# Value windows and key tiles at one distance for all tiles, and five transfers per pair issued by ScalarE

## The reference

```python
# 1: neighbourhood attention, 16 heads of 8 channels, a 7 x 7 window clamped at the image's edges
xf  = ln_c(x).transpose(0, 2, 3, 1)
q, k, v = split(xf @ qkv_w.T);  q = q * 8 ** -0.5
si = clip(arange(56) - 3, 0, 49)          # first key row of query row i; sj likewise for columns
logits[i, j, a, c] = q[i, j] . k[si[i] + a, sj[j] + c] + rpb[si[i] + a - i + 6, sj[j] + c - j + 6]
x = x + (softmax(logits over a, c) @ v) @ proj_w.T + proj_b
# 2: mixture of experts on tokens: top 2 of 8 experts, hidden width 512, relu
t = tokens(x);  t = t + moe(ln_t(t))
```

## Time and profile before

| what | us |
|---|---|
| median of three runs (lowest, highest) | 3022.98 (3019.34, 3025.69) |
| the profiled execution: its own time | 3022.68 |
| the profiled execution: span from first to last instruction | 3020.9 |
| time around the span in it | 1.8 |
| PE busy over the span | 2688.8 (89%) |
| DVE, ACT, POOL busy over the span | 2269.4, 2114.3, 1583.9 |
| mean granted clock of PE over the span | 0.947 |

### The profile page before, as it was taken

One profiled execution on the slowest core, in us unless ns is written; L12 is line 12 of the kernel. 1 busy time (PEld: TensorE's weight loads), 2 busy tenths in 40 slices (PEclk: granted clock), 3 DMA queues, 4 the chain that ended last, 5 costly groups with the idle time before them and its releaser, 6 DMA issues. The chain is left out here.

```text
span 3020.9 us, 112796 instructions
## 1 busy us (share of the span) xinstructions
PE 2688.8 (89%) x31346; PEld 2395.9 (79%) x31451; DVE 2269.4 (75%) x12559; ACT 2114.3 (70%) x5724; POOL 1583.9 (52%) x2025
## 2 busy tenths in 40 slices
PE   4789999999999999999999999999939999999733
PEld 2789999899989998999899989999936766776522
DVE  2668888788878887888788868888857888888655
ACT  1567878787878886887787868888847777777500
POOL 2135555455545554555455545555565777777600
PEclk9999999999999999999999999999969999999855
DMA  2665666555546664656566645566645444444399
GB/s 48 153 122 124 129 124 123 112 122 127 126 102 130 124 124 102 130 128 124 101 127 128 129 99 124 125 125 129 132 91 105 97 94 97 97 94 97 101 323 322
DMA packets 714047, 378.50 MB, mean 125 GB/s; under 512 B 422528, under 2 KB 669984, under 8 KB 713504
## 3 DMA queue, kind: packets, MB, share of 16 engines
q1 hardware_dynamic: 660704, 235.97, 40.3%
q10 hardware_dynamic: 24192, 81.67, 9.5%
q0 software_dynamic: 28608, 54.48, 6.1%
HBM read 233.43 MB, written 98.11 MB: 110 GB/s over the span
## 5 line engine op out<-in xcount | busy, mean ns | idle before, releaser
L1061 ACT ACTIVATE pr<-sc,nmx 128x100 f32<-128x100 f32 x3136 | 923.9, 369 | 61.9 <-DVE nmx L678 60.9
L962 POOL TENSOR_TENSOR oml<-om 128x256 f16<-128x256 f32 x784 | 479.6, 612 | 907.3 <-DVE om L708 890.4
L533 PE MATMUL bank<-vwin,pt 100*128 100x65 f32 x6272 | 806.2, 272 | 36.3 <-DVE om L708 28.1
L678 DVE CUSTOM_DVE_ANT_0 sc<-bank,near 128x100 f32<-128x100 f32 x3136 | 633.5, 257 | 253.7 <-PE bank L511 207.8
L533 PEld LDWEIGHTS bank<-vwin,pt 100*128 100x128 f32 x6272 | 773.4, 194 | 54.3 <-ACT pt L1069 39.5
L511 PE MATMUL bank<-kimg,held 128*128 (+2 forms) x9408 | 628.2, 216 | 40.9 <-issue 22.9
L511 PEld LDWEIGHTS bank<-kimg,held 128*128 128x128 bf16 (+1 forms) x9408 | 561.3, 100 | 88.3 <-issue 56.7
L1069 ACT ACTIVATE pt<-bank 100x512 f32<-100x512 f32 x784 | 460.6, 587 | 223.5 <-PE bank L520 208.8
L1367 POOL DMA_INDIRECT yrows<-ye,meta x420 | 449.2, 1070 | 154.6 <-issue 109.8
L930 POOL DMA_INDIRECT xrows<-rows,idx x448 | 433.9, 969 | 114.9 <-issue 75.5
L520 PE MATMUL bank<-cst_sb,pr 128*100 128x128 f32 x3136 | 477.1, 275 | 0.0
(11 more groups left out here) (133 smaller groups left out, 3366.8 us busy)
## 6 DMA issues: line engine op xcount, KB each, us to landing
vwin<-v_pix SPq DMA_DIRECT2D x1120, 60.5 KB
near<-bias_rows ACTq DMA_DIRECT2D x112, 600.0 KB, 4.7
y<-yrows SPq DMA_DIRECT2D x112, 224.0 KB, 4.3
held<-qring SPq DMA_DIRECT2D x896, 14.0 KB
v_pix<-vrow SPq DMA_DIRECT2D x56, 225.8 KB
xin<-in_x SPq DMA_DIRECT2D x56, 224.0 KB
xres<-in_x SPq DMA_DIRECT2D x112, 112.0 KB
x<-xres SPq DMA_DIRECT2D x112, 112.0 KB
```

The lines of the kernel that those rows point to most:

```text
L533: mm = pe.matmul(ps_av[m % 2][:, 2 * t + blk, :], pt[:, m % 2, 2 * t + blk, :], vwin[:, st, 2 * u + t, 64 * blk:64 * blk + 65], start=True ...
L678: i = v.tensor_tensor_reduce(out=sc[:, ring(m, par), k, :], in0=ps_s[m % 2][:, k, :], in1=near[:, st, ct, k, :], scale=-1.0, scalar=-MASKE ...
L962: g.tensor_tensor(oml[:, st, u], om[:, st, u], om_h[:, st, u], ALU.subtract).then_inc(s["oml_done"], 1)
L1061: i = a.activation(pr[:, r, k, :], sc[:, r, k, :], ACT.Exp, bias=nmx[:, r, k:k + 1], scale=-1.0)
```

## The change

All 14 tiles of a strip get their keys at one distance: tile t begins at column 4 t - 3, also at the edges, where it then reaches three columns beyond the image's row. What it finds there (pixels of the neighbouring row, or zeros before the first and behind the last pixel of all) is masked: the mask tables and the offset into the bias table are changed so that the edge tiles' valid keys lie where they now fall. The key image `kimg` gets 4 columns before and behind, set to zero by four DVE memsets; `v_pix` gets 4 rows before and behind, set to zero by two POOL transfers. A strip's values come by ten transfers of 14 tiles in place of ten of 12 tiles and two for the edges.

Two stores of x1, two residual loads and one token load per pair leave SP's list and go to ACT's list at units 4, 7, 11 and 13, behind that unit's `exps` and routing steps. SP's list of a pair is put in a new order.

```diff
@@ windows (SP)
-                    at = ((J // NPAIR) * IMG + krow(J, st) * W) * VW
+                    at = ((J // NPAIR) * IMG + krow(J, st) * W + EDGE - 3) * VW
                     for kr in range(KW):
-                        src = bass.AP(v_pix.tensor, at + (kr * W + 1) * VW, [[VW, KW], [TS * VW, NTILE - 2], [1, VW]])
-                        sp.dma_start(vwin[kr * KW:(kr + 1) * KW, st, 1:NTILE - 1], src).then_inc(s[f"v_in{st}"], 16)
-                    for t, c0 in ((0, 0), (NTILE - 1, W - KW)):
-                        src = bass.AP(v_pix.tensor, at + c0 * VW, [[W * VW, KW], [VW, KW], [1, VW]])
-                        sp.dma_start(vwin[:, st, t], src).then_inc(s[f"v_in{st}"], 16)
+                        src = bass.AP(v_pix.tensor, at + kr * W * VW, [[VW, KW], [TS * VW, NTILE], [1, VW]])
+                        sp.dma_start(vwin[kr * KW:(kr + 1) * KW, st], src).then_inc(s[f"v_in{st}"], 16)
@@ body (SP), for a pair J
-                    if not early(J, 1):
-                        store_x1(J - 1, 0)
+                    if more:
+                        spread_q(J + 1, 1 - par)
                     if fetch:
                         load_x(I + 1)
                     windows(J, 1, tail and J == PAIRS - 1)
                     if more:
-                        spread_q(J + 1, 1 - par)
-                    if not early(J, 1):
-                        store_x1(J - 1, 1)
-                    load_res(J, 0)
-                    if more:
                         windows(J + 1, 0, tail)
-                    load_res(J, 1)
-                    if not early(J, 1):
-                        load_tokens(J - 1, 1 - par)
                     if I is not None:
                         store_v(I)
                     if isinstance(J, int) and J == 0:
                         ...
@@ scores (PE)
-                        k0 = min(max(TS * tile - 3, 0), W - KW)
+                        k0 = TS * tile - 3
@@ start of the lists of DVE and POOL
+                for part in range(2):
+                    for col in (0, EDGE + IMG):
+                        i = v.memset(kimg[:, part, col:col + EDGE], 0.0)
+                i.then_inc(s["k_edge"], 1)
+                g.wait_ge(s["null_done"], 2)
+                for px in (0, EDGE + B * IMG):
+                    g.dma_start(bass.AP(v_pix.tensor, px * VW, [[run, lines], [1, run]]), none[0:lines, 0:run]).then_inc(s["v_edge"], 16)
@@ bias tables (DVE) and masks
-                                    o_r, o_c = 6 - 3 * rt, 6 - 3 * tt
+                                    o_r, o_c = 6 - 3 * rt, 3
-                    r, c = lo(qr, rt), lo(qc, ct)
+                    r, c = lo(qr, rt), (KW - KSZ, qc, 0)[ct]
@@ body (ACT), at the end of unit m; load_res, store_x1 and load_tokens now wait and issue on ACT
+                            if early(J, 1):
+                                if m == 0:
+                                    load_res(J, 0)
+                                    load_res(J, 1)
+                            elif m == 4:
+                                store_x1(J - 1, 0)
+                            elif m == 7:
+                                load_res(J, 0)
+                            elif m == 11:
+                                store_x1(J - 1, 1)
+                            elif m == 13:
+                                load_res(J, 1)
+                                load_tokens(J - 1, 1 - par)
```

More of the change, by code:

```diff
@@ L81 @@
 NROW = PAIR // HALF
-WIN_DMAS = 16 * (KW + 2)
+WIN_DMAS = 16 * KW
+EDGE = 4
 def build(nc, x, qkv_w_t, rpb, proj_w_t, proj_b, w_router, w1, b1, w2, b2, cst, win, cst2, out):
@@ L103, in sem @@
             return ctx.enter_context(nc.semaphore(name))
-        v_pix = nc.dram_tensor("v_pix", (B * IMG, VW), FP32, kind="Internal").ap()
+        v_pix = nc.dram_tensor("v_pix", (B * IMG + 2 * EDGE, VW), FP32, kind="Internal").ap()
         bias_rows = nc.dram_tensor("bias_rows", (3, 128, 3 * 4 * NKEY), FP32, kind="Internal").ap()
@@ L147, in build @@
         near = asb("near", [128, 2, 3, 4, NKEY])
-        kimg = asb("kimg", [C, 2, IMG], BF16)
-        kimg_h, kimg_l = kimg[:, 0], kimg[:, 1].bitcast(FP16)
+        kimg = asb("kimg", [C, 2, IMG + 2 * EDGE], BF16)
+        kimg_h, kimg_l = kimg[:, 0, EDGE:EDGE + IMG], kimg[:, 1, EDGE:EDGE + IMG].bitcast(FP16)
         qring = asb("qring", [C, QRING * 2 * STRIP])
@@ L230, in build @@
             c_small r_small r_wrm r_const r_first r_x0 r_x1 r_t r_turned r_logit r_stat r_ve r_pow r_nmr r_lg r_top r_atf r_hot r_hots
-            r_gap r_gapr r_eg r_share r_gate r_pos r_prod r_idxf r_idx r_cap r_xn r_hi r_lo r_dest r_both r_sc0 r_sc1 w2_in split_h split1 split2 t_ready null_done null_in""".split()
+            r_gap r_gapr r_eg r_share r_gate r_pos r_prod r_idxf r_idx r_cap r_xn r_hi r_lo r_dest r_both r_sc0 r_sc1 v_edge k_edge w2_in split_h split1 split2 t_ready null_done null_in""".split()
         s = {n: sem(n) for n in names}
@@ L319, in store_v @@
                     sp.wait_ge(s["v_out"], I + 1)
-                    dst = bass.AP(v_pix.tensor, I * (PAIR * VW), [[VW, HALF], [HALF * VW, NROW], [1, VW]])
+                    dst = bass.AP(v_pix.tensor, (I * PAIR + EDGE) * VW, [[VW, HALF], [HALF * VW, NROW], [1, VW]])
                     sp.dma_start(dst, vrow[:]).then_inc(s["v_store"], 16)
@@ L379, in body @@
                         if I == 1:
+                            sp.wait_ge(s["v_edge"], 32)
                             windows(0, 0, False)
@@ L435, in _ @@
                 pe.wait_ge(s["zeroed"], 2)
+                pe.wait_ge(s["k_edge"], 1)
                 pe.wait_ge(s["c_small"], 32)
@@ L891, in _ @@
                 g.memset(lost[:], 0).then_inc(s["null_done"], 1)
+                g.wait_ge(s["null_done"], 2)
+                lines = 8 if EDGE * VW % 8 == 0 else 6
+                run = EDGE * VW // lines
+                for px in (0, EDGE + B * IMG):
+                    g.dma_start(bass.AP(v_pix.tensor, px * VW, [[run, lines], [1, run]]), none[0:lines, 0:run]).then_inc(s["v_edge"], 16)
                 g.memset(ahead[:], TOK)
@@ L1046, in near_bias, with load_res, store_x1, load_tokens @@
                     a.dma_start(near[:, st].rearrange("p c a k -> p (c a k)"), src).then_inc(s[f"near_in{st}"], 16)
+                def load_res(J, st):
+                    b = J // NPAIR
+                    if not (isinstance(J, int) and J == 0):
+                        a.wait_ge(s[f"x1_store{st}"], 16 * J)
+                    src = bass.AP(x.tensor, b * (C * IMG) + (J % NPAIR) * PAIR + st * STRIP, [[IMG, C], [1, STRIP]])
+                    a.dma_start(xres[:, st, :], src).then_inc(s[f"xres_in{st}"], 16)
+                def store_x1(J, st):
+                    a.wait_ge(s["proj_out"], 2 * J + st + 1)
+                    a.dma_start(x1[:, bass.ds(J * PAIR + st * STRIP, STRIP)], xres[:, st, :])\
+                        .then_inc(s[f"x1_store{st}"], 16)
+                def load_tokens(Q, par):
+                    if not early(Q, 2):
+                        a.wait_ge(s["r_logit"], Q - 1)
+                    a.dma_start(xt[:, par, :], x1[:, bass.ds(Q * PAIR, PAIR)]).then_inc(s[f"r_x{par}"], 16)
                 def exps(J, m, par):
```

## The result

| | before | after | ratio (95%) |
|---|---|---|---|
| median, us | 3024.34 | 3075.93 | 1.0144 (1.0115 to 1.0174) |
| profiled execution, us | 3022.68 | 3067.8 | |
| its span, us | 3020.9 | 3066.0 | |

The forecast was 3030, its range ended at 3047. The sign was right, the size was not: +45.1 us of span between the two profiled executions (+51.6 between the medians), where +7.0 was summed.

The account below looks back on a forecast made before the run. PE's own list was taken to bound the loop, with SP late only at J = 1. The terms, +6.1 us at J = 1 and +0.9 at J = 0, the rest 0, gave +7.0 and 3030.0 us, range 3018 to 3047.

Parts of the forecast that it names:

- Part 2: Five issues per pair moved from SP to ACT in stage 1: 0 us, bounds 0 and 94 us.
- I take a landing under 5 us and no wait: At unit 13, the x1 store issued at unit 11 lands before ACT's residual load needs it, 5.1 us later: 0 us.
- Part 3: SP's new order, spread first: 0 in the loop, +6.1 us at J = 1, +0.9 us at J = 0.
- ACT is held at unit 13: Rival, chance 0.18: ACT's residual load waits for a late x1 store, 0.3 us in each of 53 pairs, +16 us: 3046.
- Each us of landing is a us of ACT: At unit 13, from 5.1 us on, every further us the x1 store takes to land delays ACT by one us.
- five issues at 0 us: The issues moved to ACT sit behind its exponentials and cost nothing; at most 1.7 us a pair if all exposed.
- Part 4: The edges: masks, paddings and memsets leave the other engines' work unchanged; at most 1 us, taken as 0.
- Matmuls keep their shapes and counts: At the strips' edges, matmuls, activations and vector work stay the same in shape and number, so 0 us.
- Part 1: Ten window loads in place of twelve per strip: some 200 us of SP's time saved, worth 0 us as nobody waits.
- the 2.6 us from there to PE: At J = 1, the time from the end of the window loads to PE's start, taken as 2.6 us as before.
- The first pairs don't get longer: Rival, chance 0.17 (no change): the null rows end some 6 us sooner, so the windows stay where they were: 3024.
- The spread was the late one: Rival, chance 0.13 (faster): an earlier spread ends ACT's 50.7 us of waits and PE's 16.9 us before the key projection: 3013.

Follow-up runs that it names:

- e1: The changed kernel with strip 1's x1 store issued by ACT at unit 9 in place of unit 11; ratio 1.0068 to the kernel before.
- e7: The changed kernel with the next strip's ten window loads behind the values' store in SP's list, not ahead of it; ratio 1.0646 to the kernel before.
- e3: The kernel before with only the five issues per pair moved to ACT, keeping twelve loads and SP's old order; ratio 1.0017 to the kernel before.
- e2: The changed kernel with SP's list in its old order, the spread between the two strips' windows; ratio 1.0064 to the kernel before.
- e11: The kernel before with ten loads a strip and all tiles at even columns, everything issued by SP in the old order; ratio 0.9924 to the kernel before.
- e4: The kernel before with only the ten 14-tile loads, masks and paddings added, all issued by SP in the old order; ratio 1.0064 to the kernel before.
- e8: The changed kernel with SP's list in its old order and all tiles' keys at even columns; ratio 0.9914 to the kernel before.
- e5: The changed kernel with the key image 3 columns into its buffer, not 4, so all tiles begin at even columns; ratio 1.0023 to the kernel before.
- e6: The kernel before with its key image shifted one column, so inner tiles begin at even columns and edge tiles at odd ones; ratio 0.9955 to the kernel before.

## Why the prediction was wrong

**Part 2 failed, as the rival said it could.** The step "I take a landing under 5 us and no wait" rested on the one x1 store that the trace of before showed, 1.3 us, which stands at the end of stage 1 with nothing beside it. The row itself was right for a store without neighbours: in the loop of e1 and e7, too, the last packet is over after 1.35 to 1.65 us. What was left out is what the change itself puts beside the store. By Part 3's new order SP starts the next strip's ten window loads just ahead of it, and then the last packet takes up to 6.1 us and ACT's load goes up to 7.19 us behind the store. "ACT is held at unit 13" had 0.18 and +16 us; e1 puts its price at 19. "Each us of landing is a us of ACT" was not quite so. Set beside e1 pair by pair, leaving out the pairs at and behind a jump back, the 18 pairs with a distance up to 6.3 us are no longer than there (by 0.1 us at most), and the 15 over 6.6 us are 0.5 to 1.3 us longer. So about a us of lateness is free, and the next costs more than itself, as the three issues behind the load then lie open too. The other step of Part 2, five issues at 0 us, held where nothing holds ACT (e3).

The Trainium skill (DMA: Bandwidth & Descriptors, section "Issuing engines are not separate DMA queues") says that transfers of several engines end up on the same 16 DMA engines and interleave. The trace agrees: between the first and the last packet of ACT's store at 1058.65 (1059.6 to 1064.4) run those of SP's window loads, and its last one ends 5.75 us after its issue, in e1 1.4 us after.

**Part 4 failed.** "Matmuls keep their shapes and counts" was true and not enough: 48 of a pair's 168 score matmuls belong to units with an edge tile, and half of those went from 45 to 52 ns, +0.16 us a pair, some 8 us in the loop (+8.4 and +9.4 in e1 and e2, which have little or no hold). The trace of before showed it, 0.74 beside 0.79 us a group; I had read the group's mean.

**Part 1's "worth nothing"** holds for SP's issues: e1, e2 and e11 show no gain from SP's shorter list outside the jump backs, and SP's waits for PE grew as forecast, by some 7 us a pair (6 said). For the longer jump backs of e4 and e11 (PE idle there 27.3 and 26.9 us in five, before 21.9) the cause stays open; the instructions are fetched by DMA queues too (two queues named "instruction" in the profile), but nothing here separates that.

**Part 3 held**, with one term too small. Null rows until 148.9 (148.7 said), spread 13.22 us (12.5), load of x as said, and the ten loads until some 167.4 (166.3). Only the 2.6 us from there to PE became 4.9; at J = 1 the other ten loads follow at once, which may be why, but no run separates it. PE starts at 172.27 (168.9), the first pairs cost +10.1 (+7.0), inside the bounds. In the loop its cost of 0 was wrong by its effect on Part 2: without the new order there is no hold to speak of (e2).

**The rivals.** "The first pairs don't get longer" fell with the stall. "The spread was the late one" fell too: the wait is now put down to PE, as long in all as under its two names before, and PE's own 16.9 us are still 14.7.

The sum in its measured terms: 10.1 first pairs + 8 edges + 19 hold = 37 of the 45.1 us; of the 8 us left 6.3 lie in the last stage, which the change doesn't touch.

## What to carry to other kernels

A landing time must be read where the transfer will run, with the neighbours that it will have; where the trace shows one only on empty queues, that row is a lower bound. When a wait is given to an engine with work of its own, look for what the same change puts on the queues just then, and move the transfer out of its way: two units earlier, ahead of the burst, the same store landed in 1.7 us. And compare single instances of a matmul group, edge beside middle: a mean over the group hid a difference that was worth some 8 us here, and 36 us to the kernel that has all its tiles at even columns (e8 beside e2).

## What the runs showed of the hardware

- A score matmul of 100 columns of bf16 whose rows begin at an even column took 44 to 49 ns, mostly 45, at an odd one 52 to 53 ns (0.54 and 0.63 us for twelve), in both directions (e5 with columns 4 t, e6 with 4 t - 2); one odd tile of e6 took 63 ns. The Trainium skill (TensorE: Matmul & The Clock Gate, section "Wait — 56ns, not 53.3ns?") gives columns divided by 2.4 GHz plus 2.5 ns at full clock, by which 100 columns are an estimated 44 ns: the even case agrees, the odd one does not.
- A store of 112 KB in the loop had its last packet done 1.35 to 1.65 us after its issue with no burst of another engine's loads beside it (e1, e7), and 2.6 to 6.1 us, median 5.3, with six to nine loads of 70.5 KB issued just ahead of it on another engine's queue (after).
- An idle stretch of 2.10 us on PE was followed by some 24 us at the lower clock (e7), and the same 15 us of idle time ahead of J = 0 by some 3 us or by some 25 us of it.
